# A Mamba, slot-routing, windowed-attention chain on one core: the residual stream kept in SBUF from the first slot stage to the last

## The reference

```python
x = x + mamba_block(_layernorm(x), ...)      # two Mamba layers (d_inner 512, 16 states), then a layernorm with weight w and bias b
x = x + slot_block(_layernorm(x), ...)       # "ffn"
x = x + attention(_layernorm(x), W_qkv, b_qkv, W_proj, b_proj)   # 16 heads of 16, causal window of 64
x = x + slot_block(_layernorm(x), ...)       # the same weights as the first one

def slot_block(x, slot_init, slot_scale, w1, b1, w2, b2, gru..., wv, bv, wo, bo, tau):
    S = slot_init * slot_scale                              # 64 slots, the same for each batch
    h = gelu(concat([x, mean(S)]) @ w1.T + b1)
    route_logits = (h @ w2.T + b2) / (abs(tau) + 0.1)
    topk_vals, topk_idx = top_k(route_logits, 8)
    alpha = scatter(softmax(topk_vals))                     # tokens x 64
    gi = einsum('bts,btd->bsd', alpha, x) / (alpha.sum(1) + 1e-8)
    S_new = GRU(gi, S)                                      # gates r, z, candidate n
    return einsum('bts,bsd->btd', alpha, S_new @ wv.T + bv) @ wo.T + bo
```

## Time and profile before

| what | value |
|---|---|
| median of 3 runs | 2386.9 us (2381.8 to 2387.57) |
| the profiled execution | 2384.84 us; span 2383.0 us |
| busy over the span | PE 87%, DVE 79%, ACT 75%, POOL 70% |
| granted TensorE clock, mean | 0.961 of full speed |
| mamba, f1, attention, f2: start of each | 0, 1769.6, 1904.5, 2290.2 us |
| store of 512 KB of rows, issue to landing | 2.9 us (mamba_residual<-residual) |
| store of 128 KB, issue to landing | 1.7 us (after_attention<-a_out) |

### The profile page before, as it was taken

How to read it: one execution, slowest core, us unless ns; L and a number is a source line. 1 busy time by engine, 2 the same in 40 slices (tenths; PEclk the granted TensorE clock), 3 DMA queues, 4 the chain that set the end, 5 groups by cost and what they waited for, 6 DMA issues and landing times. The chain is left out here.

```text
span 2383.0 us, 40888 instructions
## 1 busy us (share of the span) xinstructions
PE 2075.0 (87%) x14808; PEld 1245.8 (52%) x14808; DVE 1888.8 (79%) x2586; ACT 1787.2 (75%) x3059; POOL 1658.2 (70%) x1440
## 2 busy tenths in 40 slices
PE   5989898898989899898989889898745779999977
PEld 2445555454545545454555545454423557777755
DVE  6788989888888988888888989888859455666665
ACT  3998998989899898989889898988825234554542
POOL 2788889898988989898888989898957032222020
PEclk9999999999999999999999999999976879999989
DMA  7340514224050523314051422404032221110032
GB/s 238 71 114 20 125 45 99 67 67 111 24 125 17 150 67 92 89 46 115 20 125 45 98 68 67 112 23 116 18 109 93 73 74 37 33 48 22 25 129 71
DMA packets 129789, 183.83 MB, mean 77 GB/s; under 512 B 14002, under 2 KB 75954, under 8 KB 129204
## 3 DMA queue, kind: packets, MB, share of 16 engines
q1 hardware_dynamic: 129588, 181.23, 28.6%
HBM read 134.51 MB, written 42.47 MB: 74 GB/s over the span
## 5 line engine op out<-in xcount | busy, mean ns | idle before, releaser
L620 POOL TENSOR_TENSOR h<-h,C_rep 128x512 f32<-128x512 f32 x1024 | 1275.7, 1282 | 195.3 <-ACT h_carry L529 195.3
L404 DVE TENSOR_TENSOR_SCAN h<-decay,h_carry,psum 128x512 f32<-128x512 f32 x768 | 956.3, 1272 | 126.6 <-PE psum L751 93.9
L521 ACT ACTIVATE decay<-dt_rep,A 128x512 f32<-128x512 f32 x1024 | 732.6, 716 | 95.2 <-DVE h L404 91.4
L751 PEld LDWEIGHTS psum<-ident,u_B 128*128 128x128 f32 x4096 | 477.0, 141 | 561.7 <-DVE h L404 308.9
L751 PE MATMUL psum<-ident,u_B 128*128 128x128 f32 x4096 | 631.3, 280 | 141.3 <-DVE h L404 109.0
L543 ACT ACTIVATE u_B<-u_tok,B_tok 128x512 f32<-128x512 f32 x832 | 592.0, 713 | 64.3 <-PE psum L751 46.6
L404 DVE TENSOR_TENSOR_SCAN h<-decay,zero,psum 128x512 f32<-128x512 f32 x256 | 318.7, 1271 | 50.0 <-PE psum L751 34.2
L762 PE MATMUL psum<-h,state_sum 128*32 128x512 f32 x2048 | 281.4, 622 | 9.9 <-POOL h L620 9.4
L609 POOL TENSOR_TENSOR u_B<-u_tok,B_tok 128x512 f32<-128x512 f32 x192 | 200.6, 1045 | 19.1 <-DVE u_tok L375 19.1
L674 PE MATMUL psum<-x_dt_gated,tap_diag 128*128 128x512 f32 x384 | 189.2, 597 | 0.0
L1619 DVE TENSOR_REDUCE a_row_max<-a_psum 128x4 f32<-128x512 f32 x128 | 87.8, 686 | 94.6 <-PE a_psum L1761 94.6
(11 more groups left out here) (207 smaller groups left out, 2764.7 us busy)
## 6 DMA issues: line engine op xcount, KB each, us to landing
dt_rep<-dt_rows SPq DMA_DIRECT2D x256, 256.0 KB, 5.6
C_rep<-C_rows SPq DMA_DIRECT2D x256, 64.0 KB, 2.0
dt_rows<-x_dt_gated SPq DMA_DIRECT2D x32, 512.0 KB, 4.9
residual<-mamba_residual SPq DMA_DIRECT2D x16, 512.0 KB, 3.9
mamba_residual<-residual SPq DMA_DIRECT2D x16, 512.0 KB, 2.9
x_tok<-mamba_residual SPq DMA_DIRECT2D x15, 512.0 KB, 4.4
f_gru_weights<-in_slot_gru_dram SPq DMA_DIRECT2D x2, 2176.0 KB
u_B<-in_x_dram SPq DMA_DIRECT2D x8, 512.0 KB, 9.2
```

The lines of the kernel that those rows point to most:

```text
L404: dve.tensor_tensor_scan(h[:, slot(u)], dec[:, u % DEC], PS[:, u % 2], first, ALU.mult, ALU.add)\
L521: act.activation(dec[:, u % DEC], dtr[:, k % EG], ACT.Exp, scale=A[:, s // STEPS, k:k + 1]).then_inc(S["decay"], 1)
L620: pool.tensor_tensor(h[:, slot(u)], h[:, slot(u)], crep[:, k // EG], ALU.mult).then_inc(S["hc"], 1)
L751: ins = pe.transpose(PS[:, u % 2, tb * P:(tb + 1) * P], pr[:, f % 2, tb, eg], ident[:])
```

## The change

It touches four things.

1. **Last step of mamba.** POOL leaves the last three units (`LAST_V = 3`) to DVE, which multiplies them once its last scan and carry are done (`last_outputs`, semaphore `hc_v`). PE's last step is written out on its own: the out-projection of channel groups 0 and 1 comes ahead of the last two state sums, that of 2 and 3 behind them, in other PSUM banks (`last_bank`), with 4 and 5 fillers between.
2. **What stays in SBUF.** A class `Kept` holds x, r, the slot weights, identity, slots, biases, the statistics, a normalised chunk, the masks. f1 writes x in place and stores nothing; attention loads nothing and adds in place; f2 loads the GRU weights only. The attention weights are loaded in f1 into tiles of r that have been used up, and attention's v tiles live in r too. POOL adds attention's output bias in place (L1649 of the new kernel), behind the normalisation of that chunk.
3. **Moments one stage ahead.** f1 takes the moments of the first four tiles between its last additions and POOL normalises them; attention takes the moments of its own output, tile by tile (`out_stats`, `out_variance`, `out_rstd`), all but the last tile's; f2 takes that one (`late_moments`).
4. **Slot stages.** In f1 the bias of group 0 is added by DVE, those of 1 to 3 by POOL, each only after the group before it is combined. `prepare_slots` is cut into four pieces placed between the groups and between the gathers. The exponentials and `weigh` of the first three groups come ahead of the last gelu and the last `top_k`.

The core of the diff:

```diff
@@ mamba, DVE, POOL and PE, last step
+                def last_outputs():
+                    at(dve, "carry", ALL * QUADS)
+                    dve.wait_ge(c_ld[NG - 1], 16 * SG * ALL)
+                    for u in range(ALL * UNITS - LAST_V, ALL * UNITS):
+                        dve.tensor_tensor(h[:, slot(u)], h[:, slot(u)], crep[:, NG - 1], ALU.mult).then_inc(S["hc_v"], 1)
-                        if 0 <= s < ALL:
+                        if 0 <= s < ALL and s * UNITS + k < ALL * UNITS - LAST_V:
                             output(s, k)
-                    at(pe, "hc", q0 + QT)
+                    at(pe, "hc", min(q0 + QT, ALL * UNITS - LAST_V))
+                    if q0 + QT == ALL * UNITS:
+                        pe.wait_ge(S["hc_v"], LAST_V)
+                def last_step():
+                    last_out(0)
+                    last_out(1)
+                    warm(4)
+                    states(ALL - 1, QUADS - 2)
+                    warm(5)
+                    states(ALL - 1, QUADS - 1)
+                    last_out(2)
+                    last_out(3)
@@ slots, SP
+                    sp.dma_start(keep.identb[:], identb_in).then_inc(S["a_ld"], 16)
+                    sp.dma_start(keep.mask[:], mask_in).then_inc(S["a_ld"], 16)
+                    sp.wait_ge(S["xa"], 2)
+                    sp.dma_start(keep.AW, attn_pack).then_inc(S["a_ld"], 16)
+                    sp.wait_ge(S["a_ld"], 48)
+                else:
+                    sp.dma_start(RB[:], rows).then_inc(S["u_ld"], 16)
+                    sp.dma_start(U[:], gru_pack).then_inc(S["u_ld"], 16)
@@ slots, POOL
                 def add_bias(g):
+                    if g not in BIAS_P:
+                        return
                     pool.wait_ge(x_ld[g], 16)
+                    pool.wait_ge(S["xa"], g)
                     pool.tensor_tensor(xa[:, t], xa[:, t], wb[:, 1:2].to_broadcast([P, TG, D]), ALU.add).then_inc(S["x_b"], 1)
+                if normed:
+                    rstd(R_AT[0])
+                    rstd(R_AT[1])
                 for g in range(G):
                     if normed:
...
+                        add_bias(g + 1)
+                        rstd(X_AT[g])
                     norm_x(g)
+                    if normed and g + 2 < G:
+                        rstd(R_AT[g + 2])
+                    if not normed and g == 1:
+                        late_rstd()
+                if normed:
+                    attention_rows()
@@ slots, DVE
                     top_k(g)
-                for n in range(G):
-                    weigh(n)
+                    if g == G - 2:
+                        for e in range(G - 1):
+                            weigh(e)
+                weigh(G - 1)
...
+                    if normed and m == 1:
+                        dve.wait_ge(S["y"], 2)
+                        for i in range(CH):
+                            dve.bn_stats(keep.st[:, i], xa[:, i]).then_inc(S["a_st"], 1)
+                    if normed and m == 2:
+                        dve.wait_ge(S["a_st"], CH)
+                        for i in range(CH):
+                            dve.bn_aggr(keep.mv[:, i], keep.st[:, i]).then_inc(S["a_st"], 1)
+                        dve.wait_ge(S["a_st"], 2 * CH)
+                        dve.tensor_scalar(keep.ve[:, 0:CH], keep.mv[:, 0:CH, 1], EPS, None, ALU.add).then_inc(S["a_ve"], 1)
@@ slots, PE
                 for g in range(G):
                     hidden(g)
+                    if g == PREP:
+                        prepare_candidate()
+                    if g == PREP + 1:
+                        prepare_values()
                     features(g + 1)
+                    if g == G - 1:
+                        prepare_gates()
                     logits(g)
-                prepare_slots()
                 pe.wait_ge(S["hT"], 2 * G)
-                pe.wait_ge(S["pre"], 1)
+                pe.wait_ge(S["wvo"], 1)
                 for n in range(GB):
                     gather(n)
+                    if n == 0:
+                        gate_biases()
@@ attention, DVE
-                    if J >= 8:
-                        dve.wait_ge(stored[J % 8], 16 * (J // 8))
-                    dve.tensor_tensor(yo[:, J % 8], PS[:, 6, D:2 * D], xb[:, J // TG % 2, J % TG], ALU.add).then_inc(S["o"], 1)
+                    dve.tensor_tensor(xa[:, J], PS[:, 6, D:2 * D], xa[:, J], ALU.add).then_inc(S["o"], 1)
+                    J = tile_at(n, ADD + 1)
+                    if J is not None and J < NJ - 1:
+                        out_stats(J)
+                    J = tile_at(n, ADD + 2)
+                    if J is not None and J % TG == TG - 1 and J < NJ - 1:
+                        out_variance(J // TG)
@@ hybrid
+        keep = Kept(nc, ctx)
+        slots(nc, "f1_", keep, slot_gru, slot_rows, normed=(x, r, norm_w), loads=(slot_first, ident, attn_pack, ident_bf16, attn_mask))
+        attention(nc, keep)
+        slots(nc, "f2_", keep, slot_gru, slot_rows, out=out)
```

More of the change, by code:

```diff
@@ L846, with slots @@
 B_ALL = B_BO + D
-def slots(nc, tag, x, out, first_pack, gru_pack, rows, ident_in, normed=None):
+def slots(nc, tag, keep, gru_pack, rows, out=None, normed=None, loads=None):
     TG = 8
@@ L1544, in v_skew @@
                     pool.wait_ge(S["v0"], 3 * s + 3)
-                normalise(0)
                 k_halo(0)
```

467 lines of the change are left out of this document (260 added, 207 removed).

## The result

| what | before | changed |
|---|---|---|
| median, range | 2386.6 us (2381.8 to 2387.57) | 2345.83 us (2342.48 to 2347.07) |
| ratio, 95% interval | | 0.9836 [0.9818, 0.9854] |
| profiled execution's span | 2383.0 us | 2344.6 us |
| granted TensorE clock, mean | 0.961 | 0.971 |

The kernel is 1.6% faster; the forecast was 2349 (range 2338 to 2361). Of the spans' difference of 38.4 us, the stages have these parts. The column "measured" is the difference of the two profiled executions.

What follows compares the result with a forecast made beforehand. Attention was taken as TensorE-bound, f1 as DVE-bound with POOL in its way, with PE idle at stage heads. Terms summed to -37.1: 2347.7 from the profiled 2384.84, 2349.8 from the median; forecast 2349 us, range 2338 to 2361 with rivals 1 and 2.

Steps and rivals of the forecast that it cites:

- End of mamba: Mamba's tail: DVE's share of the multiplications and PE's new order at full clock end it at 1756.0; -9.0 us.
- f1 up to the gathers: f1 to the gathers' end: first normalise 3.9 us earlier, alphas 4.0 earlier, gathers end at 1870; -5.5 us.
- the slow one is another, and I change nothing: Gathers of the slot stages: one per stage still runs slow, only a different one; no change to the sum.
- Last additions and the boundary: End of f1: bn_stats and small instructions add +2.2 us; the store gone before attention gives -5.4.
- Head of attention: Attention's opening: PE's first transposes have all they need at once; 18.75 us to first scores stay; -9.9 us.
- now starts with the stage: Attention's head: DVE's 6.9 us memset starts at the opening and ends as q does, 7 us in.
- Inside attention: Attention: DVE's 18.5 us of added moments are mostly taken up by its waits for PE; +1 us.
- Rival 4: Attention: DVE's later answers make the clock fall to 1.2 GHz; half the stage gives +177, 2526; chance 0.03.
- Attention to f2, and f2: Boundary: less to land, -1.5 us; f2: first transposes 2.3 us after opening, gathers at 55; -9.0 us.
- Rival 1: Mamba's tail stays at half clock, its term is 0: 2358 us; chance 0.12.
- Rival 2: f1 and f2: table change, early `weigh` and moved products lose half of 14.5 us: 2356; chance 0.10.
- Rival 3: Attention: all 18.5 us of moments land between a shift and the next scores: 2367 us; chance 0.08.

Runs made afterwards that it cites:

- v3: v1 plus f2's first rows normalised in attention, bias rows ahead of the first gather, and PE fillers at three places of f1; 2344.62 us.
- v1: Changed kernel with half of q's tile sharing a kept tile, cleared by POOL in f1 instead of by DVE at attention's head; 2343.43 us.

## Why the prediction was right, and where its steps were not

**End of mamba** (-9.0, measured -8.8). The last addition ends at 1756.16; I had 1756.0. Two of its reasons were off. DVE's first multiplication took 3.89 us and not 0.69, since it waited for all that POOL still had to do; this changed nothing, as PE's last sum came later. And the cover is PE's order alone: without the fillers the clock holds, and without DVE's help the end was no later, in an execution in which POOL stood 1.8 us further on.

**f1 up to the gathers** (-5.5, measured -8.7): the mis-sized term. The step that failed is "the slow one is another, and I change nothing". I let one gather per stage run at half clock, from rows of one execution. In the changed kernel's execution both of f1's gathers had the full clock. In this execution and in those of eleven experiments (the late weighing, with its own pause, left out), f1's two gathers both took 3.70 seven times, and one of them took 4.38 to 5.78 five times. So a slow gather is a matter of the execution, and a forecast for a median would count about half of one. Over the six executions in which nothing of f1 up to the gathers is changed they end at 97.34 to 100.76, 99.2 at the mean: -6.8. Of the 3.2 us by which the term was off here, the alphas are 1.0 (all there 92.0 us after the opening, 93.0 forecast), the gather's clock is 1.35 (3.70 against 5.05), and for some 0.8 no run shows a cause. By the Trainium skill (TensorE: Matmul & The Clock Gate, What's actually happening) activity releases the throttle, and the sum by it would have been nearer here. But f2's second gather fell to half clock right behind 6.6 us in which PE never paused, and v3's first behind 13.8 us with one pause of 0.4. The measurement decides: neither "one gather is slow" nor "a busy PE is fast" holds.

What stands ahead of the fall can be told. In the changed kernel's execution and those of the experiments but two (the late weighing and the late `prepare_slots`, whose order on PE is another) there are 22 pairs of gathers in f1 and f2, and 12 have a slow one. Nine of these come behind the products of bias rows (one row of input) and the transposes that follow, with no pause; three (in f1 with POOL's memsets behind DVE's, in f2 with group 0's bias on POOL and with the store back) right behind PE's wait of 1.46 to 1.47 us for the last alphas. But the same rows and the same wait stand ahead of gathers that ran at full clock, so neither is shown to be the cause, and no run takes the bias rows out. It stays open.

```profile
2307.00:2309.40 2.40, 2.40 (x8) 1.00 (x6) 1.68 (x4) 0.02 (x1) 0.00 (x0) 0.95 0.00 0
2309.40:2315.60 6.20, 6.20 (x42) 4.09 (x42) 0.00 (x0) 1.19 (x2) 0.00 (x0) 0.74 0.01 3
```

The other steps of this term stood. Normalises come 3.5 to 3.6 us earlier in all four groups, -3.9 forecast for the first. The fourth `top_k` starts exactly where it did, 85.9 us after the opening: the three `weigh` and the table change in front of it used up the gain, and what pays is that nothing but one `weigh` follows it.

**Last additions and the boundary** (+2.2 and -5.4; measured +1.8 and -5.4). Four bn_stats and the five small ones cost a little less than their lengths. POOL's rows end at 1881.86 and the last addition at 1881.79: the tie that was forecast.

**Head of attention** (-9.9, measured -8.6). The transposes start 0.04 us after the opening. The step that failed is that the memset "now starts with the stage": it starts 1.78 later, which makes it the last thing q's DMAs wait for. The kernel before had the same delay ahead of it, 1.66 us, so this could have been read beforehand. v1 takes it away and gets 1.4 back.

**Inside attention** (+1, measured +2.0). Within what executions differ by, so that the single us forecast is not tested. PE's waits for DVE's shift went from 11 to 13 times and from 11.3 to 9.0 us (against the earlier trace rows); the doubled moments put 31 more instructions of this kind at 2.4 us. Rival 4 had no ground: the clock in attention is 0.98.

```profile
PE a_psum L1896 <- DVE a_probs L1765: 9.0, 13, 0.7
```

**Attention to f2, and f2** (-1.5 and -9.0; measured -1.9 and -8.8). First transposes 2.14 us after the opening, gathers' end at 55.07 and 55 forecast, with one slow gather as in the sum. In the other executions with f2 unchanged they end at 52.7 to 55.3, so the close hit is in part luck.

**The total.** The gathers of f1, better than forecast by 3.2, and the head of attention and its inside, worse by 1.3 and 1.0, partly cancel. Either side alone would have stayed inside the range.

**The rivals.** Rival 1 fell with the tail's full clock. Rival 2 holds for one part only: in f2 the new order gained nothing beside the earlier start; in f1 it gained 3 to 5 us. Rival 3 fell with the doubled moments.

## What to carry to other kernels

Work that is moved earlier on one engine takes with it the cover of a wait on another: here early weighing or cut-up products alone are 15 to 21 us slower than both, and both together gained 3 to 5 us in f1 and nothing in f2. Where two engines lock each other out, the sign is an instruction much longer than others of its shape that ends just after the other engine's; ordering them by a wait can be worth more than moving one (3.1 us against 1.0 here). A group's mean or total hides this: look at its shortest and longest instruction. To size an edit of a microsecond, count from the event that releases the path and not from the opening of the stage, since a DMA's landing moves by more than that. When a stage's head is emptied, list all that the next step waits for, small memsets included, and give none of them the earliest start for certain.

## What the runs showed of the hardware that I had not expected

- The memset of 128 x 8192 on DVE starts 1.66 to 1.78 us after DVE is free, in the profile as "issue": first in its stage or behind other work, with POOL busy or quiet. Other first instructions of DVE start after 0.07 us.
- At the end of mamba, pauses of PE of 1.31 and 1.38 us left the clock at 1.00. In f1 of the changed kernel, after pauses of 3.3 and 3.4 us, the next eight transposes ran at half (1.97 and 1.94 us); in the run with all ten multiplications on POOL, after one of 2.8 us, at full (1.09).
- The clock also fell to half in work with no pause, four times of twelve at one of f1's gathers, each time in the bias rows or within 1.1 us behind them, and once behind a pause of 1.47 us. Fillers ahead did not prevent it.
- DVE gets no turn between POOL multiplications that follow each other. In all twelve executions in which DVE multiplies at the end of mamba, its first multiplication takes 2.03 to 3.89 us, and its other two 0.68; POOL's keep their 1.23 us.
